# One transfer for the angles and sines, one normalisation fewer in the sine table, and two low parts of weights moved into the first chunk

## The reference, cut to what matters

```python
x = L0_attn_u                                  # (16, 512, 128) float32
x = x + _layernorm(attn(_layernorm(x)))        # state-space mixer
x = x + _layernorm(ffn(_layernorm(x)))         # 8 experts, all of them for every token

def attn(u):                                   # kernel[t] = eig ** t, 64 states
    Bu = einsum('btd,nd->btn', u, B_w)
    eig = (1 - 1j * omega) / (1 + 1j * omega)  # omega: imaginary part of an FFT of 32 parameters
    h = real(causal convolution of kernel and Bu along the 512 steps)
    return einsum('btn,dn->btd', h, C_w) + D * u

def ffn(x):
    h = silu(x @ w_gate[e]) * (x @ w_up[e])    # for each expert e of 8, 128 -> 512
    return sum_e cw[..., e] * (h @ w_down[e])  # cw: product of two softmaxes, normalised
```

## Time and profile before

| | before |
|---|---|
| median of 3 runs | 1120.1 us (1119.98 to 1120.21) |
| the profiled execution | 1119.97 us |
| its span, first to last instruction | 1118.2 us |
| PE busy | 1100.1 us, 98% of the span |
| DVE busy | 918.4 us, 82% |
| ACT busy | 743.5 us, 66% |
| POOL busy | 702.4 us, 63% |

### The profile page before, as it was taken

How to read it: one execution, slowest core, us unless ns; L and a number is a source line. 1 busy time by engine, 2 the same in 40 slices (tenths; PEclk the granted TensorE clock), 3 DMA queues, 4 the chain that set the end, 5 groups by cost and what they waited for, 6 DMA issues and landing times.

```text
span 1118.2 us, 16871 instructions
## 1 busy us (share of the span) xinstructions
PE 1100.1 (98%) x4807; PEld 896.9 (80%) x4807; DVE 918.4 (82%) x1779; ACT 743.5 (66%) x1430; POOL 702.4 (63%) x885
## 2 busy tenths in 40 slices
PE   8999999999999999999999999999999999999997
PEld 4677888888888888888888888888888888888885
DVE  7799888797888979888897888979888897887855
ACT  6676676757667576676757667576676757666563
POOL 1586765748567485765748567585766748556453
PEclk9999999999999999999999999999999999999999
DMA  4340413213142222313213132232313313231110
GB/s 137 96 120 13 114 48 82 79 40 104 39 102 69 67 70 63 96 47 92 72 40 100 44 100 66 69 75 52 101 48 96 75 40 94 47 87 48 48 48 20
DMA packets 182333, 79.66 MB, mean 71 GB/s; under 512 B 124608, under 2 KB 160096, under 8 KB 182240
## 3 DMA queue, kind: packets, MB, share of 16 engines
q1 hardware_dynamic: 182240, 78.57, 26.2%
HBM read 59.14 MB, written 19.40 MB: 70 GB/s over the span
## 4 chain that ended last, share of the span: by engine, by line
PE 92%; DVE 4%; ACT 1%; issue 1%; POOL 0%; DMA 0%; POOLq 0%; ACTq 0%; SPq 0%; DVEq 0%
PE u L372 10%; PE u L374 10%; PE g L372 10%; PE u L373 10%; PE g L374 10%; PE g L373 10%; PE y L372 10%; PE y L374 10%; PE y L373 10%; DVE hid L1029 1%; ACT gate L691 0%; DVE hid_lo L1035 0%; PE n_ps L465 0%; PE n_ps L466 0%; PE m_ps L372 0%
## 5 line engine op out<-in xcount | busy, mean ns | idle before, releaser
L1349 POOL TENSOR_TENSOR hid_lo<-hid,hid_hi 128x512 fp32r<-128x512 f32 x255 | 333.5, 1308 | 339.4 <-ACT hid_hi L697 339.4
L691 ACT ACTIVATE gate<-g 128x512 f32<-128x512 f32 x512 | 305.9, 598 | 315.2 <-PE g L374 314.4
L1029 DVE TENSOR_TENSOR hid<-gate,u 128x512 f32<-128x512 f32 x512 | 348.3, 681 | 179.3 <-ACT gate L691 142.4
L697 ACT ACTIVATE hid_hi<-hid 128x512 fp32r<-128x512 f32 x512 | 320.0, 625 | 32.4 <-DVE hid L1029 30.7
L1035 DVE TENSOR_TENSOR hid_lo<-hid,hid_hi 128x512 fp32r<-128x512 f32 x257 | 217.8, 848 | 0.2
L372 PE MATMUL u<-xe_hi,w_hi 128*128 128x512 f32 x512 | 200.0, 391 | 1.6 <-DVE hid L1029 1.5
L372 PE MATMUL g<-xe_hi,w_hi 128*128 128x512 f32 x512 | 199.6, 390 | 0.1
L374 PE MATMUL u<-xe_hi,w_lo 128*128 128x512 f32 x512 | 199.3, 389 | 0.0
L372 PE MATMUL y<-hid_hi,w_hi 128*128 128x512 f32 x512 | 199.3, 389 | 0.0
L374 PE MATMUL g<-xe_hi,w_lo 128*128 128x512 f32 x512 | 199.3, 389 | 0.0
L373 PE MATMUL g<-xe_lo,w_hi 128*128 128x512 f32 x512 | 199.3, 389 | 0.0
(11 more groups left out here) (234 smaller groups left out, 1168.7 us busy)
## 6 DMA issues: line engine op xcount, KB each, us to landing
cw_b<-cw_scratch SPq DMA_DIRECT2D x128, 256.0 KB, 3.3
x_sb<-x_in SPq DMA_DIRECT2D x16, 256.0 KB, 3.1
out_scratch<-acc_t SPq DMA_DIRECT2D x60, 64.0 KB, 1.9
ffn<-out_scratch SPq DMA_DIRECT2D x15, 256.0 KB, 2.7
x_out<-o_sb SPq DMA_DIRECT2D x15, 256.0 KB, 2.2
xn_scratch<-mix_t SPq DMA_DIRECT2D x56, 64.0 KB, 2.2
feat<-xn_scratch SPq DMA_DIRECT2D x14, 256.0 KB, 2.6
y_scratch<-mix_t SPq DMA_DIRECT2D x56, 64.0 KB, 1.9
```

The lines of the kernel that those rows point to most:

```text
L691: nc.scalar.activation(gate[:, k % 2, :], g_ps[k % 2][:], ACT.Silu).then_inc(gate_ready, 1)
L697: nc.scalar.activation(hid_hi[:, slot(c, k), :], hid[:, slot(c, k), :], ACT.Copy).then_inc(hi_ready, 1)
L1029: nc.vector.tensor_tensor(hid[:, slot(c, k), :], gate[:, k % 2, :], u_ps[k % 2][:], ALU.mult).then_inc(hid_ready, 1)
L1349: nc.gpsimd.tensor_tensor(hid_lo[:, slot(c, k), :], hid[:, slot(c, k), :], hid_hi[:, slot(c, k), :].bitcast(f32), ALU.subtract).then_inc(l ...
```

## The change

The parameters and the sine rows are one array of 32 rows by 129 columns, so SP issues one transfer where it issued two. The normalisation of the one-step pair (`unit(1)`) is gone; that of the four-step pair (`unit(4)`) stays. The three mean-and-variance links of x, which ran in the shade of `unit(1)`, stand in the doubling levels of one and two, and the shift of x, which stood in the level of one, stands in the level of eight. The low parts of pieces 10 and 11 leave the opening: PE makes them behind units 1 and 2 of chunk 0, and ACT keeps them there, with `y_ps[0]` and `y_ps[1]` as their PSUM tiles.

```diff
+EARLY_LO = 10
+        def lo_home(n):
+            return (g_ps[0], u_ps[0], y_ps[0])[n % 3] if n < EARLY_LO else y_ps[n - EARLY_LO]
...
-            sp.dma_start(a_col[:], a_in).then_inc(angle_loaded, 16)
-            sp.dma_start(sines[:], sines_in).then_inc(angle_loaded, 16)
+            sp.dma_start(angles[:], angles_in).then_inc(angle_loaded, 16)
...
-            pe.wait_ge(angle_loaded, 32)
-            nc.tensor.matmul(m_ps[:, 0:1], sines[:], a_col[:], start=True, stop=True).then_inc(omega_ready, 1)
+            pe.wait_ge(angle_loaded, 16)
+            nc.tensor.matmul(m_ps[:, 0:1], angles[:, 0:P], angles[:, P:], start=True, stop=True).then_inc(omega_ready, 1)
...
-            for n in range(2 * PIECES, AHEAD * PIECES - 1):
+            for n in range(2 * PIECES, EARLY_LO):
                 make_lo(n)
             early_turn_xe()
-            make_lo(AHEAD * PIECES - 1)
...
+                    if first and 1 <= k <= 2:
+                        make_lo(EARLY_LO + k - 1)
...
-            keep_lo(10)
             early_hi_xe()
-            keep_lo(11)
...
+                    if first and 1 <= k <= 2:
+                        keep_lo(EARLY_LO + k - 1)
...
-            unit(1, lambda: mean_var_1(stats, mv, var_eps, mix_link, 0), lambda: mean_var_2(mv, var_eps, mix_link, 0),
-                 lambda: mean_var_3(mv, var_eps, mix_link, 0).then_inc(var_ready, 1))
+            steps_x = {(1, 0): [lambda: mean_var_1(stats, mv, var_eps, mix_link, 0)],
+                       (1, 1): [lambda: mean_var_2(mv, var_eps, mix_link, 0)],
+                       (2, 0): [lambda: mean_var_3(mv, var_eps, mix_link, 0).then_inc(var_ready, 1)],
+                       (8, 0): [early_shift_x]}
...
-                then(nc.vector.tensor_scalar(v_sin[:, old], low[:, 0, old], si, None, ALU.mult))
-                if n == 1:
-                    early_shift_x()
+                then(nc.vector.tensor_scalar(v_sin[:, old], low[:, 0, old], si, None, ALU.mult),
+                     *steps_x.get((n, 0), ()))
```

More of the change, by code:

```diff
@@ L97, in lo_count, with build @@
     return sum(on_pool(j) == on_pool(k) for j in range(k + 1))
-def build(nc, x_in, proj_in, a_in, sines_in, d_in, wgate_in, wup_in, wdown_in, out):
+def build(nc, x_in, proj_in, angles_in, d_in, wgate_in, wup_in, wdown_in, out):
     f32, f32r = mybir.dt.float32, mybir.dt.float32r
@@ L130, in build @@
         minus = sb("minus", [P, P], f32r)
-        a_col, sines = sb("a_col", [NS // 2, 1]), sb("sines", [NS // 2, P])
+        angles = sb("angles", [NS // 2, P + 1])
         d_col = sb("d_col", [P, 1])
@@ L383, in make_lo @@
                 e, cols = n // PIECES, slice(n % PIECES * F, (n % PIECES + 1) * F)
-                dst = (g_ps[0], u_ps[0], y_ps[0])[n % 3]
+                dst = lo_home(n)
                 pe.wait_ge(w_hi_done, n + 1)
@@ L569, in keep_lo @@
                 act.wait_ge(lo_made, n + 1)
-                nc.scalar.activation(w_lo[:, e, cols], (g_ps[0], u_ps[0], y_ps[0])[n % 3][:], ACT.Copy).then_inc(w_lo_act, 1)
+                nc.scalar.activation(w_lo[:, e, cols], lo_home(n)[:], ACT.Copy).then_inc(w_lo_act, 1)
             def early_norm_x():
@@ L1099, in _ @@
                 then(nc.vector.scalar_tensor_tensor(out=low[:, 1, new], in0=low[:, 1, old], scalar=co,
-                                                    in1=v_sin[:, old], op0=ALU.mult, op1=ALU.add))
+                                                    in1=v_sin[:, old], op0=ALU.mult, op1=ALU.add),
+                     *steps_x.get((n, 1), ()))
                 n *= 2
@@ L1429 @@
         "proj_in": np.concatenate([b_t, b_t, np.concatenate([c_t, c_t], axis=0), L0_ffn_w_router, L0_ffn_w_gating], axis=1),
-        "a_in": np.asarray(L0_attn_a_params).reshape(NS // 2, 1),
-        "sines_in": sine_rows(),
+        "angles_in": np.concatenate([sine_rows(), np.asarray(L0_attn_a_params).reshape(NS // 2, 1)], axis=1),
         "d_in": np.asarray(L0_attn_D).reshape(D, 1),
```

## The result

| kernel | median, us | runs | span and mean clock of the profiled run |
|---|---|---|---|
| before | 1120.1 | 7, 1119.92 to 1120.60 | 1118.2, 0.998 |
| after | 1123.03 | 7, 1122.47 to 1124.89 | 1120.9, 0.996 |

The ratio is 1.0026, 95% interval 1.0016 to 1.0036: the change made the kernel slower by 2.9 us. The time lies inside the predicted range, but 1.6 us above the forecast; by the prediction's own bound of 2.24 us it is "slower", which had a chance of 0.32, and not "no change", which had 0.64. The seven runs fall into two groups: four from 1122.47 to 1123.03 with a mean clock of 0.994 to 0.996, and three from 1124.14 to 1124.89 with 0.993. The profiled run (1122.83) is of the first group.

A forecast was written before the change was run, and what follows sets the result against it. PE, busy every microsecond from 105 to 1085 us, was taken as the bound. First unit +0.67 and chunk 0 +0.6 gave +1.27 us on 1119.97, with 0.1 to the median: 1121.4, range 1119.6 to 1123.6.

The forecast's parts named there:

- the prediction's own bound of 2.24 us: About 0.2% of the kernel's time: the smallest difference that a measurement was taken to tell from no change.
- The transfer: Start of the opening: one transfer instead of two saves an issue step, so work starts 0.45 us earlier.
- The shift of x: Opening, DVE: shift at 8.5 instead of 7.50, so ACT's normalisation of x starts 1.05 us later, at about 8.75.
- the table's gain dying at PE: Opening: table 2.15 us earlier, but PE reaches C at 19.8 to 20.0 instead of 20.02; gain 0 to 0.2 us.
- the rival with 0.08: Opening: POOL's power holds DVE's table, opening 1.0 us longer still, total 1122.4 us; chance 0.08.
- y's layer norm +0.85: Opening, ACT: the pass of y's layer norm moves from 24.74 by 0.85 us, carried to the first unit.
- The end of the opening -0.18: Before the first unit: piece 10's copy no longer precedes xe's high halves, saving 0.18 us, bounds 0 and 0.5.
- Chunk 0 +0.6: Chunk 0: two low parts add 2.16 us of PE work, mostly absorbed by waiting; net cost 0.6 us.
- the rival that had 0.15: Chunk 0 takes up all the added work and gains 1.2 us, total 1119.6 us; chance 0.15.
- under 2.3: Sign that the prediction is right: PE's gaps up to 105 us total under 2.3 us instead of 3.36.
- The clock: Rival: PE idles 2.4 us ahead of x's transposes, clock falls, 1.5 us lost, total 1122.9 us; chance 0.12.
- two rivals: The clock falls ahead of x's transposes, or chunk 0 takes up nothing: each 1122.9 us, each with chance 0.12.

The follow-up runs named there:

- section 8: Low parts in the opening: the change with shift of x in level 4, 1120.45 us; with statistics first, 1119.68; kernel before with one transfer only, 1119.68.
- the table above: Lists xn, request for expert 3, first unit and median of the kernel before, the three kernels of section 8 and section 1; medians 1119.68 to 1121.12 us.
- section 2: Kernel before with only low parts 10 and 11 moved into chunk 0: 1122.74 us, ratio 1.0018.
- section 1: The change with low parts 10 and 11 back in the opening: 1121.12 us, ratio 1.0007.
- section 6: The change plus eight warming matmuls ahead of the transposes of xe and four behind, 1122.56 us; with five more ahead of low part 9 (three places), 1123.25.
- section 7: The change plus warming matmuls: eight ahead of the transposes of xe, four behind, and eleven instead of seven ahead of those of xn: 1121.14 us, ratio 1.0007.
- section 5: The change with low part 10 back in the opening, ahead of the transposes of xe (first kernel, 1122.98 us) or behind them (second kernel, 1123.56 us).
- section 3: The change with the shift of x in level 4 of the table instead of level 8: 1122.50 us, ratio 1.0017.
- section 4: The change plus five warming matmuls between low part 9 and the transposes of xe: 1122.30 us, ratio 1.0019.

## Why the prediction was half right

**The transfer** was forecast at -0.45; the first product on PE is 0.48 earlier. Right.

**The shift of x** at 8.5, xn at 8.75, **the table's gain dying at PE**, C at 19.8 to 20.0, no gain: right to 0.1 us, and section 8 shows it by runs. It was also right that the power does not hold DVE: the rival with 0.08 fell. The rule of the Trainium skill, "SBUF — State Buffer", section "SBUF: two separate sides", would have had DVE's instructions with two SBUF inputs stand still for the 1.03 us of the power; the trace disagrees for these, which take 0.21 and 0.22 with the power and without it.

**y's layer norm +0.85** was too small: it came at 26.12, +1.38. The request for expert 3 was 0.98 later, as worked out, but the high parts behind its landing were 1.57 later. From the request to these high parts it took 4.19 before and 4.78 after; over the kernels of the table above and the kernel after it goes from 4.2 to 4.8 without a pattern that I can name. This term has an uncertainty of 0.6 that the step left out; its cause stays open.

**The end of the opening -0.18** came as 1.46 - 1.38 = +0.08. The copy's absence did help: in section 2, from y's pass (24.87) to the first unit (31.59) it is 6.72, where it was 6.90, just the 0.18. But in the kernel after the transposes ran at half clock (0.48 in place of 0.33 each) and took it back.

**Chunk 0 +0.6** was wrong. It takes up both low parts whole, -0.13 to 0: the rival that had 0.15, though without the further gain it came with. PE's idle time in the stretch fell from 1.93 to 0.93, less than the 2.16 of work that was added; from the first unit to the product that stood at 105 before, PE is idle for 2.57, where the prediction's sign was "under 2.3" in place of 3.36. A matmul's row is 0.39 long and its pace is 0.23, so each pause hides up to 0.16 behind the row ahead of it; that this makes up the rest is argued, not shown.

**The clock** is the step that failed. The rival was there, with 0.12, but for one wait only, the one ahead of the transposes of x. That same prediction took one low part out of PE's list ahead of the transposes of xe and one from behind them, booked 0.18 us for it, and did not ask how long PE would then stand: ahead of the transposes the waits of section 1 (0.56 and 1.19) and the part's own 1.3 become one wait of 3.08, and behind them it waits 0.98. The working asked of each moved instruction what it costs where it lands, not what it held up where it stood. For the wait it did look at, the mechanism was right and the price too (1.5 forecast, 1.6 measured). But its length was not: the seven warming matmuls ran until 9.10 in the profiled run and left 1.28, not 2.4. In the profile of the kernel with three places filled (section 6) they took 4.71 instead of 6.08 and left 2.65: the median row took 429 ns and not 634, so the clock had risen earlier. The Trainium skill, "TensorE: Matmul & The Clock Gate", section "What's actually happening", has activity as what releases the clock; the runs agree, 0.998 or more in 11 of 11 once PE is kept at work (section 7). So one profile tells this wait badly, and whether the clock falls behind it varies from run to run. The same section says that the point at which the clock changes varies from run to run; the warming matmuls, with 4.71 to 6.26 us for the same list, bear that out for the rise, and the two groups of runs fit it. That it fell there in the three longer runs of the kernel after is inferred from sections 5 and 7; none of the three was profiled.

The sum, by the runs: 0.7 to 0.8 us for the late xn (sections 1 and 7), about 2 for the clock in the first unit and the transposes ahead of it (1122.9, the middle of the first group after, less the 1121.14 of section 7, is 1.8; each against its own before, 2.1), and 1.7 more in three of seven runs. The forecast had the first (0.67), left out the second, held the third unlikely, and added 0.6 for chunk 0 that did not come. That the median of 1123.03 lies next to 1122.9, the price of two rivals, is luck: chunk 0 took up all of the work, and the fall that the profile of the first group shows is not at the place that the rival named. The range held the time only because these two rivals had stretched it.

## What to carry to other kernels

Before work is moved off an engine, ask what it held up there: on PE, a low part that nobody waits for can be what keeps the clock. Where a shortened chain ends in a list that another chain feeds (here C behind the low parts), it is worth nothing, and the move that pays for it (here the shift, later by three levels) is paid in full. When the times of a kernel stand in two groups, look at the mean clock beside each before explaining the median (section 6: 0.997 or 0.998 in the faster group, 0.996 or 0.997 in the slower).

## What the runs showed of the hardware

- The granted clock went from 1.00 to 0.50 inside a wait of 3.08 us in the kernel after, in section 3 and in the second kernel of section 5; in section 2, with the same wait, it fell at 31.0, behind the transposes that followed it. It also fell behind 1.76 once, and in the first unit behind waits of 0.92 and 0.98 (section 4) or 1.19 and 1.15 (the first kernel of section 5) with four transposes between them; it did not fall behind 2.33 and 2.65 in the profiled runs of section 6, nor in the kernel before, with 1.20 and a low part between transposes and first unit. So the length of the last wait alone doesn't decide it.
- The clock of the same kernel falls in some executions and not in others: going by the groups, in six of 11 for either kernel of section 6, with 1.5 to 1.7 us between the groups. Another kernel with the same opening (section 1) has two of 11 runs (1122.61 and 1123.32) that stand apart in the same way, and of the many runs of the kernel before beside the sections at least three do (1122.05, 1122.09 and 1122.13, each with a mean clock of 0.996). With PE kept at work through both stretches (section 7) all 11 runs have a mean clock of 0.998 or 0.999.
- Warming matmuls that only multiply the identity count as work for this: eight and four of them, and four more ahead, gave back about 2 us (1123.03 to 1121.14).
- At the start, the seven warming matmuls took from 4.71 to 6.26 us in kernels whose list is the same up to there: a row of them takes 634 ns before the rise and 379 after it, so the time at which the clock rises differs by over 2 us between executions (an estimate: at twice the rate, 1.55 us less means a rise some 3 us earlier).
